# Expert stage written out without its loop, waits carried by the indirect transfers, and the first pair of experts finished before the second is prepared

## What is computed

```python
logits = xf @ gate_w.T                                   # 64 experts
top_scores, top_idx = jax.lax.top_k(sigmoid(logits), 2)   # two experts for each row
top_scores = 2.5 * top_scores / (top_scores.sum(-1, keepdims=True) + 1e-20)
pos = running count of the rows of each expert, CAP = 256
buf = zeros((64, 256, 128)).at[flat_e, pos].set(x_pairs, mode='drop')
h = silu(einsum('ecd,edh->ech', buf, w1)) * einsum('ecd,edh->ech', buf, w3)
y = einsum('ech,ehd->ecd', h, w2)
routed = (y of both experts of the row, 0 past CAP, times top_scores).sum(axis=1)
out = h + shared(xf) + routed
```

## Time and profile before

| | us |
|---|---|
| median of 3 runs | 1717.03 |
| lowest, highest | 1716.64, 1719.13 |
| the profiled execution, its own time | 1715.9 |
| its span, first to last instruction | 1714.0 |
| stage one, until POOL's last scatter starts | 1450.4 |
| first transfer of POOL's that adds to the output | 1466.2 |
| last one | 1709.0 |

### The profile page before, as it was taken

One profiled execution on the slowest core, in us unless ns is written; L12 is line 12 of the kernel. 1 busy time (PEld: TensorE's weight loads), 2 busy tenths in 40 slices (PEclk: granted clock), 3 DMA queues, 4 the chain that ended last, 5 costly groups with the idle time before them and its releaser, 6 DMA issues.

```text
span 1714.0 us, 31340 instructions
## 1 busy us (share of the span) xinstructions
PE 1519.8 (89%) x9222; PEld 1169.7 (68%) x9222; DVE 1470.9 (86%) x6005; ACT 1187.7 (69%) x1997; POOL 1273.1 (74%) x1162
## 2 busy tenths in 40 slices
PE   2699999999999999999999999999999981776661
PEld 1477777777777777777777777777777760555551
DVE  2489999999999999999999999999999982886671
ACT  2898888888888888888888888888888740111110
POOL 0018777777777777787777777777777776688888
PEclk9899999999999999999999999999999986898885
DMA  8886666666666666665656566555555111576653
GB/s 132 216 218 140 142 140 137 132 131 124 124 118 120 112 119 112 113 111 110 110 110 111 113 112 110 112 113 113 114 113 111 42 25 45 99 114 89 101 78 34
DMA packets 259939, 193.51 MB, mean 113 GB/s; under 512 B 65514, under 2 KB 239269, under 8 KB 259785
## 3 DMA queue, kind: packets, MB, share of 16 engines
q1 hardware_dynamic: 206008, 173.23, 49.7%
q0 software_dynamic: 51200, 17.87, 8.7%
q10 hardware_dynamic: 2576, 0.60, 0.3%
HBM read 84.34 MB, written 83.73 MB: 98 GB/s over the span
## 4 chain that ended last, share of the span: by engine, by line
PE 72%; POOL 15%; issue 6%; ACT 3%; DVE 2%; DMA 1%; ACTq 1%; SPq 0%; POOLq 0%
PE bank L855 11%; POOL out_rows L602 10%; PE bank L915 8%; PE bank L932 8%; PE bank L1002 5%; PE bank L879 4%; PE bank L1010 4%; PE bank L892 4%; PE bank L863 4%; POOL slot_rows L561 3%; PE bank L974 3%; PE bank L969 2%; PE bank L964 2%; PE bank L986 2%; PE bank L953 2%
## 5 line engine op out<-in xcount | busy, mean ns | idle before, releaser
L561 POOL DMA_INDIRECT slot_rows<-xs,slot x768 | 869.3, 1132 | 241.2 <-issue 240.9
L619 ACT ACTIVATE img<-img 84x980 f32<-84x980 f32 (+1 forms) x192 | 342.2, 1784 | 17.5 <-DVE wcol L1203 13.1
L855 PE MATMUL bank<-img,w_tok 126*128 126x392 f32 (+1 forms) x640 | 224.2, 497 | 11.1 <-DMA img<-img 11.0
L602 POOL DMA_INDIRECT out_rows<-img,etok x128 | 199.5, 1559 | 30.0 <-issue 29.2
L855 PEld LDWEIGHTS bank<-img,w_tok 126*128 126x128 f32 (+1 forms) x640 | 122.9, 192 | 95.2 <-issue 14.7
L688 ACT ACTIVATE xs<-h,nb,rs 128x128 f32<-128x128 f32 x384 | 154.7, 482 | 18.4 <-DVE nb L1257 11.2
L915 PE MATMUL bank<-pos_a,v 128*128 128x325 f32 (+2 forms) x768 | 158.7, 355 | 1.3 <-ACT gt L758 1.3
L701 ACT ACTIVATE xh<-h,nb,rs 128x128 f32<-128x128 f32 x384 | 154.0, 482 | 1.0 <-DVE nb L1230 0.9
L932 PE MATMUL bank<-a_t,v 128*128 128x325 f32 (+2 forms) x768 | 152.0, 346 | 0.0
L539 POOL TENSOR_TENSOR rs<-ve,neg_half 128x6 f32<-128x6 f32 x64 | 87.3, 1365 | 81.2 <-DVE ve L1225 81.1
L915 PEld LDWEIGHTS bank<-pos_a,v 128*128 128x128 f32 (+1 forms) x768 | 125.1, 190 | 30.5 <-ACT gt L758 1.7
(11 more groups left out here) (203 smaller groups left out, 3711.0 us busy)
## 6 DMA issues: line engine op xcount, KB each, us to landing
img<-in_x SPq DMA_DIRECT2D x384, 150.1 KB
img<-img SPq DMA_DIRECT2D x256, 160.8 KB
img<-img SPq DMA_DIRECT2D x128, 128.6 KB
out_rows<-fin SPq DMA_DIRECT2D x128, 128.0 KB
slot_rows<-xs,slot POOLq DMA_INDIRECT x768
slot_rows<-init_rows SPq DMA_DIRECT2D x16, 540.0 KB, 9.5
img<-slot_rows SPq DMA_DIRECT2D x32, 270.0 KB
h<-in_txt SPq DMA_DIRECT2D x64, 128.0 KB, 2.2
```

What stands on the lines that cost most here:

```text
L561: g.indirect_dma_start(out=slots_d, out_offset=bass.IndirectOffsetOnAxis(ap=slot[0:nt, q.x, r, part:part + 1], axis=0), in_=xs[0:nt, q.x, ...
L602: g.indirect_dma_start(out=out, out_offset=bass.IndirectOffsetOnAxis(ap=etok[:, q.load, m:m + 1], axis=0), in_=ysum[:, q.load, m, :], in_o ...
L619: a.activation(cols[:, b0:b0 + nb, :], raw[:, q.u, :].rearrange("p (t b) -> p b t", b=P)[:, b0:b0 + nb, :], ACT.Copy)\
L855: ins = mm(bank[:, 7, 0:2 * PATCHES], w_tok[r, m, :], xk[r, k.u, :, m, :], start=(m == 0), stop=(m == SHIFT - 1))
```

## The change

Three edits, which touch POOL and DVE and, through the loop, all engines in stage two.

1. `expert_pairs` calls the body 32 times in a row. All pairs have fixed numbers, all waits are for constants. The work of a pair is the same.
2. POOL's additions into `spare` and the semaphores `p_go`, `e_sparea` and `e_spareb` are gone, 64 in stage one and 64 in stage two. What they waited for else is waited for by the first transfer behind them.
3. DVE does `weighted(0)` and `finish_even(0)` before `prepare(1)`; for all other pairs the order stays.

```diff
 def expert_pairs(eng, body):
-    turns = E // 8
-    for m in range(4):
-        body(Experts(0, m))
-    with eng.Fori(1, turns - 1) as j:
-        for m in range(4):
-            body(Experts(j, m))
-    for m in range(4):
-        body(Experts(turns - 1, m))
+    for n in range(E // 2):
+        body(Experts(n // 4, n % 4))
...
                 if first(q):
                     pool.wait_ge(s_init, 16 * (SLOTS // 1024 + 1))
-                wait(pool, S["p_go"], q, 1)
 
                 pool.wait_ge(S["v_slot"], q.count())
-                g.tensor_tensor(out=spare[:, 2:3], in0=neg_half[:, 0:1], in1=neg_half[:, 1:2], op=ALU.add)\
-                    .then_inc(S["p_go"], 1)
...
-                for e, (ready, passed) in enumerate((("e_ya", "e_sparea"), ("e_yb", "e_spareb"))):
+                for e, ready in enumerate(("e_ya", "e_yb")):
                     wait_expert(pool, X[ready], q)
-                    wait_expert(pool, X[passed], q, 1)
                     wait_expert(pool, e_add[e], q, 1, 32)
-
-                    g.tensor_tensor(out=spare[:, e:e + 1], in0=neg_half[:, 0:1], in1=neg_half[:, 1:2], op=ALU.add)                        .then_inc(X[passed], 1)
                     for m in (2 * e, 2 * e + 1):
                         g.indirect_dma_start(
...
                 if is_first(q):
                     prepare(q)
                     gated(q)
+                    weighted(q)
+                    finish_even(q)
                 if not is_last(q):
                     prepare(q.next())
                 if not is_first(q):
                     finish_odd(q, 1)
                 if not is_last(q):
                     gated(q.next())
-                weighted(q)
-                finish_even(q)
+                if not is_first(q):
+                    weighted(q)
+                    finish_even(q)
```

More of the change, by code:

```diff
@@ L385, in program @@
             a_d0 a_d1 a_d2 a_h a_xh a_xt a_th0  a_abs a_sin a_qs a_g a_x2 a_x2t a_lgt a_sl a_lg a_small
-            p_rs1 p_rs2 p_go""".split()
+            p_rs1 p_rs2""".split()
         S = {n: sem(n) for n in names}
-        enames = """e_tr e_xt e_z e_silu e_g e_y0 e_sel e_wd e_wm e_w e_cur e_sparea e_spareb e_ya e_yb e_comb e_sum
+        enames = """e_tr e_xt e_z e_silu e_g e_y0 e_sel e_wd e_wm e_w e_cur e_ya e_yb e_comb e_sum
             e_rows e_prep e_psum e_same e_pm e_place e_mate e_mt e_kept e_move e_tok""".split()
```

## The result

| | before | after |
|---|---|---|
| median, us | 1717.88 (22 runs) | 1715.34 (22 runs) |
| lowest to highest | 1715.59 to 1721.95 | 1711.15 to 1720.43 |
| ratio, 95% interval | | 0.9984 (0.9976 to 0.9992) |
| the profiled execution, its span | 1715.9, 1714.0 | 1716.2, 1714.4 |

The change saves 2.7 us (1.4 to 4.1). 1710.1 us was predicted from 1717.0, so 6.9 us. The direction was right and the time lies inside the range, but 4 of the 6.9 us are missing, and they are the subject here. (The landing of a transfer is the moment at which its semaphore tells that the data has arrived; a landing of 5 us comes 5 us after the transfer's start on POOL.)

The account below looks back on a forecast made before the run. POOL's issue of output transfers was taken to set the end of stage two, PE bounding stage one. Savings of 5.9 + 0.8 + 0.2 = 6.9 us from 1717.0 gave 1710.1 us, range 1707.0 to 1717.0.

Parts of the forecast that it names:

- The additions of stage two: POOL's output transfers: without an addition the gap between halves falls from 0.39 to 0.30 us at 62 places, saving 5.9 us.
- The wait queue: POOL in stage two: a transfer's own wait is resolved behind the running transfer, so the 5.9 us saving stands.
- The gap stays: Rival, POOL in stage two: a transfer with its own wait still starts 0.39 us after the last; 1716.0 us, chance 0.13.
- the slower rival: Stage two: a waiting transfer isn't made ready behind the running one, gaps 0.52 to 0.73 us; 1730 us, chance 0.11.
- The additions of stage one: POOL's scatters late in stage one: four additions removed there save 0.2 to 1.1 us, taken as 0.8 us.
- if the gap is 0.30 us it saves 0.43: First late place in stage one, 1380.84 us: without the addition, 0.73 us before the next transfer would become 0.30.
- The first pair: Start of stage two: the first transfer comes 2.45 us earlier, but only 0.2 us (-0.1 to 0.5) reaches the end.
- idle for some 2 us: Sign of being right: POOL idles about this long before the third output transfer of stage two.
- The forecast third transfer: Sign of being right: the third output transfer starts 9.4 us after the start of `result(0)`, 9.55 before.
- The loop: Stage two, all engines: removing branch, registers and computed waits costed at nothing; up to 0.9 us better if DVE were on the path.
- The spare of 2.1 us at the landing: Stage two: a half's transfer needs the previous pair's landing at 7.4 us, and it lands at 5.3 us.
- The landing takes over: Rival, stage two: landings of 5.4 instead of 3.4 us become common, pace stays about 7.6 us; 1715.5 us, chance 0.05.

Follow-up runs that it names:

- e1: The changed kernel with TensorE, VectorE, ScalarE and SyncE kept in their loop, POOL written out without additions; 1709.46 us, 0.9958 of the kernel before.
- e5: e1 with VectorE's order at the first pair as before the change; 1713.60 us, 0.9967 of the kernel before.
- e9: e1 plus seven 16 KB memory-to-memory copies started by SyncE to imitate arriving code; 1711.95 us, 0.9961 of the kernel before.
- e10: e1 with SyncE's loop written out too; 1711.08 us, 0.9960 of the kernel before.
- e15: e1 run again, unchanged; 1707.38 us, 0.9954 of the kernel before.
- e4: The kernel before without the 64 additions of stage one, nothing else; 1716.83 us, ratio 1.0001 (0.9993 to 1.0010).
- e3: The kernel before with only the first pair's weighted and finish_even moved ahead of the second's prepare; 1717.32 us, ratio 1.0006.
- e2: The kernel before with only its loop written out on all engines, additions and DVE order kept; 1719.86 us, ratio 1.0018.
- e6: e1 with DVE's loop written out too; 1714.27 us, 0.9968 of the kernel before.
- e7: e1 with PE's loop written out too; 1712.97 us, 0.9961 of the kernel before.
- e8: The changed kernel with odd pairs' adds sent to a second tensor, so POOL waits for the pair before last; 1712.57 us, 0.9960 of the kernel before.
- e12: The changed kernel run again, unchanged; 1715.73 us, 0.9983 of the kernel before.
- e14: e1 with PE and SyncE written out, DVE and ScalarE in the loop; 1711.94 us, 0.9977 of the kernel before.

## Why the prediction was right or wrong

- **The additions of stage two, 5.9 us: right.** Gaps are 0.30 us with and without a wait on the transfer, and the stretch in e1, e5, e9, e10 and e15 is 232.1 to 232.4 us, 6.6 us less than 238.96. The excess over 5.9 is mostly the irregular 0.4 us of the earlier trace rows, which I had left in. (63 steps of 1.86 us are 117.2 us and not 117.3, which changes nothing.)
- **The wait queue: right.** POOL passes a transfer's wait under the running one, by the row (0.30 us) as by the Trainium skill (Perfetto Trace Analysis, DMA Instruction — SWDGE (GPSIMD)). "The gap stays" and the slower rival fall: the ordinary gap at a boundary between halves is 0.30, and the transfer itself is no longer than before. What the slower rival feared shows only where a release comes late: 0.76 us behind a landing.
- **The additions of stage one, 0.8 us: not told by the time, roughly right by the rows.** e4's interval reaches from 1.2 us faster to 1.7 us slower. The two late places gave 0.10 and 0.42 us, the low end of the 0.5 to 0.9 forecast for them. The step "if the gap is 0.30 us it saves 0.43" was wrong for the first of them: a late release costs a scatter 0.78 us without any addition, because the wait sits on a register instruction. And the earlier trace rows show PE without idle time until 1220 us, not until 1340.
- **The first pair, 0.2 us: right in its shape.** POOL waited 2.50 us for `finish_odd(0)` ("idle for some 2 us"), and e3 gave nothing that can be measured. A late transfer of stage two paid 0.28 us, inside 0.1 to 0.7. The forecast third transfer, 9.4 us after `result(0)`, came at 8.65 (9.17 in e1); but e2 had 8.56 in the old order, so that is not the new order's work.
- **The loop, 0: this is the step that failed.** It was costed "at nothing", with "Longer straight code costs PE nothing in stage one, where it is busy throughout". That looked at whether the fetching engine stalls, and it didn't. It didn't look at the landings, on which POOL waits with little to spare, and of which some of those that meet an arriving block of code came only after 5.0 to 6.0 us. Taken as a saving, the term measured about -4.5 to -5 us instead of 0 to +0.9. The Trainium skill (Runtime: NRT & Kernel Launch, Instruction fetch mechanics) calls the crossing into a new block of code mostly hidden and says that kernels prefer full unrolling. The first holds for TensorE and DVE here (e6, e7, e8 lose nothing measurable by it); the second had the wrong sign for this kernel: e2 is 1.0018.
- **The spare of 2.1 us at the landing** rested on one row of 3.4 us, and the prediction itself had a landing of 5.4 us at 1489.51. Also the time from landing to transfer, 0.76 us, was left out of it. The room is 4.8 us after the second transfer's start, so the spare over an ordinary landing is 1.4 us and not 2.1. The landings ahead of the changed kernel's gaps took 5.16 to 5.98 us, those of e12 5.0 to 5.7. "The landing takes over" named the right wait, for the wrong reason (the closer transfers, which e1 excludes), and got 0.05.
- Sum: with the loop kept, 6.9 us were forecast by the other terms and 7.2 (e1) and 7.9 (e15, 0.46% of 1717) measured. The change as made has 2.7. That 1715.3 us is inside the range is owed to its width: the upper part was there for the rivals, not for a loss through the loop.

## What to carry to other kernels

Writing out a loop is not free because no engine stalls: count the blocks of code that the instruction queues on the page of the profile will add, and ask which landing has the least room while they come. Where a wait for a landing seems to have 2 us to spare, take the spare from the worst landing in the trace, not from one typical row, and take off what lies between landing and start. And cost the parts of a combined edit one by one on the chip: here the part thought neutral took back two thirds of what the useful part gave.

## What the runs showed of the hardware

- A wait for DVE's semaphore that is part of an indirect transfer costs nothing when it is met in time (0.30 us of gap, as without one) and 0.28 us after a late release. With a wait of the sequencer ahead of the transfer it is 0.76 us from a late landing (1.49 us at the 61st transfer), with a wait on a register instruction 0.78 us.
- SyncE can take 2.7 to 3.1 us to start two loads in place of 1.0 while a block of code arrives (changed kernel, e14; 1.9 to 2.3 in e7).
- An adding transfer of 128 rows lands 3.4 us after its start (median). Landings over 4.8 us, up to 6.1, were seen only where a 16 KB block of code began to arrive 0.9 to 3.6 us after that start: 31 of 78 such cases, none of 976 others.
